# Attention over a paged cache: values gathered straight from their pages, six units turned on TensorE

## The chip, the cores and the metric

One core of a Trainium2 chip. The metric is the device time in microseconds; 3 runs of the kernel before give a median of 1006.95 us (1004.21 to 1007.05).

## The reference

Two residual layers on x (8 batches, 128 positions, 512 channels, float32):

```python
x = x + einsum('bsi,boi->bso', x, weight[adapter_ids])       # layer 0
q, k, v = x @ Wq.T, x @ Wk.T, x @ Wv.T                       # 32 q heads, 8 k/v heads, D = 128
q, k = rope(rmsnorm(q)), rope(rmsnorm(k))
kc, vc = k_cache[block_table], v_cache[block_table]          # 16 pages of 32 keys for each batch
scores = q . [kc, k] / sqrt(D), masked from cache_seqlens on
out = softmax(scores) . [vc, v]
x = x + out @ Wo.T
```

The page table, the adapter numbers and the cache lengths are inputs, known only on the chip. Each batch sees 512 cached keys and 128 new ones.

## The kernel before

**Units.** A unit u is one k/v head and one batch: hk, b = divmod(u, 8), 64 units. A unit has 4 query heads (g = 0 to 3), 640 keys (5 tiles t of 128) and two 512 x 512 weight products. Every float32 product is made as three products of float32r halves: a rounded upper part (ScalarE, a copy; names in h) and what is left (VectorE or GpSimd, a subtraction; names in l).

**Periods.** The program is written out by hand as a software pipeline. In period i TensorE makes `scores(i, g)`, projects q and k/v of unit j = i+1, multiplies the probabilities of unit w = i-1 by the values (`times_v`) and projects the output of unit o = i-2 (`project_o`). The order on each engine is the order of the calls. The first loop (periods -1 to NA) also has layer 0's products for batches 1 to 7. S, the PSUM tensor of the scores, is single, so `scores(i, g+1)` waits for `largest(i, g)`.

**Turning the probabilities.** Units below NA = 8 are normed and turned by 20 TensorE transposes (`turn_p`), and `p_hi`, `p_lo` split them out of PSUM. From unit 8 on the probabilities are cut into an upper float16 plane (`upper_plane`, ScalarE) and a lower one (`lower_plane`, VectorE, four per unit; g = 2 and 3 come one period later), and SP's DMA transposes turn both; `p_hi` (ScalarE) and `p_lo` (GpSimd, L591) read the turned planes. The last unit is turned on TensorE again.

**Keys and values.** Units 0 to NL-1 = 8 take keys straight from the pages with 16 DMAs each (`load_kt`) and values with 4 indirect DMAs of 64 KB each from GpSimd's queue (`gather_v`, L562). For the rest SP and ScalarE copy pages into an internal HBM tensor `cache_rows`, keys and values of the heads still to come, 16 pages per batch, at the pace of COPY_SP and COPY_ACT (groups of 4 pages for each period). `load_k` and `load_v` read from it, 256 KB each. From unit 8 on keys and values have one buffer, since the other half of `raw` holds the upper planes.

**GpSimd's order in a period of the second loop:** a weight split if one is due (`split_w(i, 0)`), `keys_lo(j)` (L570, kl), `q_sum(j)` (L617, m: the two rope products added, after which TensorE's `turn_q(j)` may start), `values_hi(w)` (L602, vh), `scales(j)` (L632 and L635, var and rst), `values_lo(w)` (L570, vl), three `p_lo`, a weight split if due (`split_w(i, 1)`, L570, wl), two `p_lo`.

**VectorE's order there:** `largest(i, 0)` (L1052), `lower_plane(w, 2)` (L1080), `q_products(j)` (L1115, L1119), `lower_plane(w, 3)`, `largest(i, 1)`, `output_lo`, the new value and key parts, `largest(i, 2)`, `k_sum` (L1150, waits for `scales`), `lower_plane(i, 0)`, `q_lo`, `largest(i, 3)`, the new key, `lower_plane(i, 1)`, `add_output` (L1166).

**SP's order there:** the second pair of transposes of unit i-1, the mask, weights, page copies (L338), `load_v(i)` (L443), the first pair of transposes of unit i, each released by the planes that it turns (L458, L470). The periods in which GpSimd has a split in slot 0 and in slot 1 come from the table LO_POOL and repeat with every head.

## Time and profile before

| | |
|---|---|
| median of 3 runs | 1006.95 us |
| profiled execution, first to last instruction | 1006.6 us |
| TensorE busy | 994.3 us (99%) |
| VectorE busy | 861.5 us (86%) |
| ScalarE busy | 810.3 us (80%) |
| GpSimd busy | 795.8 us (79%) |
| DMA queue of SP and ScalarE's copies and loads (q1) | 143.20 MB, 68.9% of 16 engines' span |

The page gives no time of the profiled execution other than its span; the median of the runs lies 0.35 us above it. Busy time is a mean over the whole span. The second loop makes up more than 800 us of it, with the same work in nearly every period, so one or two of its periods, read instruction by instruction, stand for it. A recorded duration includes the time that an instruction waited inside its engine for a port.

### The profile page before, as it was taken

The page shows a single profiled execution, that of the slowest core. Times are in us where ns is not written, and L with a number is a line of the kernel's source. Part 1 is how long each engine was busy: PE and PEld are TensorE (multiplying, and loading weights), DVE is VectorE, ACT ScalarE, POOL GpSimd, SP SyncE. Part 2 cuts the span into 40 slices and gives each one's busy share as a digit, 9 for nine tenths or more (in the row PEclk, how much of TensorE's full clock was granted, in tenths as well). Part 3 has the DMA queues.
Part 4 walks back from the last instruction along what each step waited for, and adds up shares of the span by engine and source line. Part 5 has one row for each costly group of instructions (what it writes and reads, how often), then busy time and mean ns, then how long its engine had stood idle before and what let it go on. Part 6 is the DMA issues. An engine that isn't in the chain of part 4 may idle for free.

```text
span 1006.6 us, 19441 instructions
## 1 busy us (share of the span) xinstructions
PE 994.3 (99%) x5471; PEld 864.3 (86%) x5471; DVE 861.5 (86%) x1787; ACT 810.3 (80%) x2109; POOL 795.8 (79%) x811
## 2 busy tenths in 40 slices
PE   8999999999999999999999999999999999999998
PEld 6778888888888888888888888888888888888886
DVE  7676657799999899999998999899999999998995
ACT  4455456698889889888988898898888988988884
POOL 4876677497889879897898888898798978888672
PEclk9999999999999999999999999999999999999999
DMA  8999879899988888888988888888988879888873
GB/s 254 277 262 260 283 229 258 213 211 201 221 162 162 161 158 153 166 157 152 171 153 162 156 160 165 148 168 155 170 148 165 157 151 166 162 162 144 153 149 84
DMA packets 513643, 180.94 MB, mean 180 GB/s; under 512 B 429873, under 2 KB 495682, under 8 KB 513538
## 3 DMA queue, kind: packets, MB, share of 16 engines
q1 hardware_dynamic: 381280, 143.20, 68.9%
q10 hardware_dynamic: 131106, 34.15, 15.3%
q0 software_dynamic: 1152, 2.36, 0.8%
q8 instruction: 45, 0.74, 0.3%
q14 instruction: 60, 0.49, 0.2%
HBM read 105.45 MB, written 31.86 MB: 136 GB/s over the span
## 4 chain that ended last, share of the span: by engine, by line
PE 95%; DVE 2%; ACTq 1%; issue 1%; ACT 1%; another core or an unknown queue 0%; POOL 0%; DVEq 0%
PE S L1408 22%; PE O L1341 7%; PE O L1343 7%; PE O L1342 7%; PE Q L1341 6%; PE Q L1343 6%; PE Y L1341 6%; PE Q L1342 6%; PE Y L1343 6%; PE Y L1342 6%; PE T L1347 4%; PE KV L1342 3%; PE KV L1341 3%; PE KV L1343 3%; PE KV L1361 1%; PE Y L1361 1%
## 5 line engine op out<-in xcount | busy, mean ns | idle before, releaser
L1080 DVE SCALAR_TENSOR_TENSOR pr<-pr,rc,raw 128x640 f16<-128x640 f32 x220 | 258.8, 1177 | 15.3 <-ACT raw L817 8.3
L1052 DVE CUSTOM_DVE_ANT_0 pr<-S,mask,rst 128x640 f32<-128x640 f32 x256 | 225.4, 881 | 16.6 <-PE S L1408 13.3
L837 ACT ACTIVATE pr<-pr,nb 128x640 f32<-128x640 f32 x256 | 211.7, 827 | 14.5 <-DVE nb L1052 14.5
L817 ACT ACTIVATE raw<-pr,rc 128x640 f16<-128x640 f32 x220 | 176.2, 826 | 0.6 <-DVE rc L1068 0.4
L617 POOL TENSOR_TENSOR m<-m 128x512 f32<-128x512 f32 x63 | 112.5, 1786 | 73.7 <-DVE m L1119 69.8
L591 POOL TENSOR_SCALAR ptl<-first 128x512 fp32r<-128x512 f16 x140 | 111.8, 799 | 17.6 <-issue 6.0
L570 POOL TENSOR_TENSOR kl<-raw,kh 128x512 fp32r<-128x512 f32 x64 | 97.8, 1528 | 34.5 <-ACT kh L720 33.5
L1408 PE MATMUL S<-kh,qh 128*128 128x320 f32 x512 | 120.8, 317 | 3.7 <-DVE nb L1052 3.6
L591 POOL TENSOR_SCALAR ptl<-turned 128x512 fp32r<-128x512 f16 x135 | 108.3, 802 | 11.2
L1408 PE MATMUL S<-kh,ql 128*128 128x320 f32 x512 | 116.8, 309 | 0.0
L783 ACT ACTIVATE Q<-Q 128x128 f32<-128x128 f32 x256 | 68.2, 266 | 59.9 <-DVE m L1119 59.9
L1408 PE MATMUL S<-kl,qh 128*128 128x320 f32 x512 | 116.2, 308 | 0.0
L1408 PEld LDWEIGHTS S<-kh,qh 128*128 128x128 f32 x512 | 91.7, 189 | 23.8 <-issue 4.7
L1341 PE MATMUL O<-pth,vh 128*128 128x512 f32 x252 | 105.5, 419 | 0.8 <-DVE ptl L983 0.5
L1341 PE MATMUL Y<-wh,oh 128*128 128x512 f32 x252 | 104.7, 415 | 0.4 <-DVE ol L983 0.4
L1341 PE MATMUL Q<-wh,xh 128*128 128x512 f32 x256 | 101.5, 396 | 0.5 <-issue 0.5
L1343 PE MATMUL Q<-wh,xl 128*128 128x512 f32 x256 | 100.9, 394 | 0.0
L1342 PE MATMUL Q<-wl,xh 128*128 128x512 f32 x256 | 100.2, 391 | 0.0
L1342 PE MATMUL Y<-wl,oh 128*128 128x512 f32 x252 | 99.7, 395 | 0.0
L1343 PE MATMUL Y<-wh,ol 128*128 128x512 f32 x252 | 99.6, 395 | 0.0
L1343 PE MATMUL O<-pth,vl 128*128 128x512 f32 x252 | 99.2, 394 | 0.0
L1342 PE MATMUL O<-ptl,vh 128*128 128x512 f32 x252 | 98.6, 391 | 0.0
(179 smaller groups left out, 2674.9 us busy)
## 6 DMA issues: line engine op xcount, KB each, us to landing
wraw<-in_wall SPq DMA_DIRECT2D x74, 256.0 KB, 4.4
cache_rows<-in_kv ACTq DMA_DIRECT2D x80, 224.0 KB
raw<-cache_rows SPq DMA_DIRECT2D x57, 256.0 KB, 4.0
raw<-cache_rows ACTq DMA_DIRECT2D x53, 256.0 KB, 5.0
mask<-mask_rows SPq DMA_DIRECT2D x64, 128.0 KB
cache_rows<-in_kv SPq DMA_DIRECT2D x36, 224.0 KB
first<-in_lw SPq DMA_DIRECT2D x5, 1024.0 KB
cache_rows<-in_kv SPq DMA_DIRECT2D x16, 192.0 KB, 4.2
```

What stands on the lines that cost most here:

```text
L570: return e.tensor_tensor(dst, src, hi.bitcast(F32), ALU.subtract)
L591: e.tensor_scalar(ptl[:, i % 3, :].rearrange("p (g n) -> p g n", g=G), plane_tile(u, 1, t), 1.0 / PS, 1.0, ALU.mult, ALU.mult).then_inc(g_ ...
L617: e.tensor_tensor(m1[:, :, :], m1[:, :, :], m2[:, :, :], ALU.add).then_inc(q_added, 1)
L783: made = e.activation(part, part, ACT.Square, accum_out=ssq[:, j % 2, r:r + 1])
L817: e.activation(upper16[:, g, :], pr[:, slot(u, g), :], ACT.Copy, scale=rc[:, u % 2, g:g + 1]).then_inc(a_f1, 1)
L837: e.activation(pr[:, slot(u, g), :], pr[:, slot(u, g), :], ACT.Exp, bias=nb[:, u % 2, g:g + 1], scale=-1.0, accum_out=sm[:, u % 2, g:g + 1 ...
L1052: e.tensor_tensor_reduce(pr[:, slot(u, g), :].rearrange("p (a n) -> p a n", a=2), S[:, :, 0:320], mask[:, u % 2, :].rearrange("p (a n) -> ...
L1080: e.scalar_tensor_tensor(out=lower16(u, g), in0=pr[:, slot(u, g), :], scalar=rc[:, u % 2, g:g + 1], in1=upper16[:, g, :], op0=ALU.mult, op ...
L1341: e.matmul(dst, lh, rh, start=first, stop=False)
L1342: e.matmul(dst, lh, rl, start=False, stop=False)
L1343: return e.matmul(dst, ll, rh, start=False, stop=last)
L1408: made = e.matmul(S[:, a, 0:320], l[:, u % 2, qs], r[:, u % 2, 320 * a:320 * a + 320], start=first, stop=last)
```

## The change

- NA goes from 8 to 6: units 0 to 5 and the last are turned on TensorE. NL is NA + 1 = 7: units 0 to 6 take their keys straight from the pages.
- All 64 units take their values from the pages, each with one indirect DMA of 256 KB (128 rows of 2 KB: four keys' values each). `load_v` is gone.
- To fit these rows, key t of a row goes to tile t: keys, mask and values are in the order (t, page, row) in place of (page, row). The host lays the caches out so, and `keys_hi` and `keys_lo` read the raw keys in runs of eight elements.
- The copies hold keys alone, 7 heads (8 for batch 7) of 16 KB per page, with new COPY_SP and COPY_ACT.
- On GpSimd `values_hi` and `values_lo` stand ahead of `q_sum` in the second loop, and behind `q_sum`, ahead of `scales`, stands the gather for unit i, after a wait for the fourth `lower_plane` of unit i-1.
- The row numbers for the gathers are made by VectorE, one instruction for each head (`value_rows`), in periods 1 to 4.

```diff
-NL = NB + 1
-NA = 8
+NA = 6
+NL = NA + 1
-COPY_SP = (0, 1, 1, 1, 1, 1, 1, 2, 0, 1, 1, 1, 1, 1)
-COPY_ACT = (2, 2, 3, 2, 2, 3, 3, 2, 1, 0, 0, 0, 0, 0)
+COPY_SP = (0, 1, 1, 1, 1, 1, 1, 2, 2, 2, 2, 1)
+COPY_ACT = (2, 3, 3, 3, 3, 3, 0, 0, 0, 0, 0, 0)
...
         def copy_page(e, b, k, number):
-            rows = slice(2 if b >= NL - NB else 4, 2 * NK)
+            rows = slice((NL - b + NB - 1) // NB, NK)
...
-            def gather_v(v, t):
+            def gather_v(v):
+                e.wait_ge(c_kidx, v // NB + 1)
+                if v >= 2:
+                    e.wait_ge(g_vlo, v - 1 if v <= NA else v)
                 e.indirect_dma_start(
-                    out=rawv[raw_at(v)][:, t, :], out_offset=None,
+                    out=rawv[raw_at(v)].rearrange("p t d -> p (t d)"), out_offset=None, in_=vc,
+                    in_offset=bass.IndirectOffsetOnAxis(ap=kidx[:, v:v + 1], axis=0)
                 ).then_inc(d_rawv[v % 2], 16)
...
-                minus(kl[:, j % 2, 0:512], rawk[raw_at(j)], kh[:, j % 2, 0:512]).then_inc(g_kc, 1)
+                minus(tiles_of(kl[:, j % 2, 0:512]), by_tile(rawk[raw_at(j)]),
+                      tiles_of(kh[:, j % 2, 0:512])).then_inc(g_kc, 1)
...
             for i in range(NA + 1, NU + 1):
                 split_w(i, 0)
                 if nxt:
                     keys_lo(j)
+                values_hi(w)
+                values_lo(w)
+                if nxt:
                     q_sum(j)
-                values_hi(w)
+                if i < NU:
+                    e.wait_ge(v_f2, G * (w - NA) + G)
+                    gather_v(i)
                 if nxt:
                     scales(j)
-                values_lo(w)
                 if w < LAST:
                     for t in range(3):
                         p_lo(w, t)
...
-                rounded(kh[:, j % 2, 0:512], rawk[raw_at(j)]).then_inc(a_kc, 1)
+                rounded(tiles_of(kh[:, j % 2, 0:512]), by_tile(rawk[raw_at(j)])).then_inc(a_kc, 1)
```

## Rows read from the trace of the kernel before

**Rows 1.** Stretches: length, then busy us (instructions) of each engine, TensorE clock, DMA.

```profile
169.12:185.84 16.72, 16.72 (x102) 14.93 (x102) 11.31 (x26) 9.61 (x30) 10.23 (x13) 1.00 0.94 267
185.84:201.72 15.88, 14.70 (x87) 12.70 (x86) 12.59 (x26) 11.68 (x29) 7.26 (x6) 1.00 0.81 169
289.10:303.62 14.52, 14.52 (x82) 12.79 (x82) 13.17 (x28) 12.34 (x32) 10.53 (x12) 1.00 0.85 156
303.62:318.14 14.52, 14.52 (x82) 12.79 (x82) 13.11 (x28) 13.17 (x34) 13.45 (x14) 1.00 0.91 172
```

**Rows 2.** Chain of waits, 160 to 180 us: start, length, what.

```profile
170.00 0.87 PE T L1347 x8
```

**Rows 3.** Who waited for whom, 230 to 970 us: total, times, longest.

```profile
POOL m L617 <- DVE m L1119: 60.9, 28, 2.3
```

**Rows 4.** SP's queue in order of time, 200 to 208 us: start, length.

```profile
204.26 2.88 SPq L338 DMA_DIRECT2D cache_rows<-in_kv  x4
```

**Rows 5.** The transposes of the lower planes (line 470): issue to landing.

```profile
DMA to landing us min/median/max: 3.3/3.4/5.3
```

**Rows 6.** The gathers (line 562): duration ns min/median/max.

```profile
L562 POOL DMA_INDIRECT raw<-in_kv,kidx x32: 943/996/1222, 12.5 to 158.8; - x32
```

**Rows 7.** GpSimd in order of time, 297 to 318 us: start, length, idle before.

```profile
297.70 1.30 POOL L570 TENSOR_TENSOR kl<-raw,kh 128x512 fp32r<-128x512 f32 x1 [0.94 <-ACT kh L720]
301.34 1.87 POOL L617 TENSOR_TENSOR m<-m 128x512 f32<-128x512 f32 x1 [2.33 <-DVE m L1119]
303.18 0.61 POOL L602 TENSOR_SCALAR vh<-raw 128x512 fp32r<-128x512 f32 x1
...
304.39 1.18 POOL L635 TENSOR_TENSOR rst<-var,mhalf 128x5 f32<-128x5 f32 x1
305.54 1.30 POOL L570 TENSOR_TENSOR vl<-raw,vh 128x512 fp32r<-128x512 f32 x1
306.92 2.48 POOL L591 TENSOR_SCALAR ptl<-turned 128x512 fp32r<-128x512 f16 x3
...
312.72 1.30 POOL L570 TENSOR_TENSOR wl<-wraw,wh 128x512 fp32r<-128x512 f32 x1
313.98 1.89 POOL L570 TENSOR_TENSOR kl<-raw,kh 128x512 fp32r<-128x512 f32 x1
315.98 1.87 POOL L617 TENSOR_TENSOR m<-m 128x512 f32<-128x512 f32 x1
```

**Rows 8.** VectorE in order of time, 298 to 318 us.

```profile
298.37 1.31 DVE L1080 SCALAR_TENSOR_TENSOR pr<-pr,rc,raw 128x640 f16<-128x640 f32 x1
...
301.18 0.88 DVE L1080 SCALAR_TENSOR_TENSOR pr<-pr,rc,raw 128x640 f16<-128x640 f32 x1
...
306.17 0.82 DVE L1150 CUSTOM_DVE_ANT_0 k<-k,rst 128x128 f32<-128x128 f32 x1
...
313.63 1.07 DVE L1080 SCALAR_TENSOR_TENSOR pr<-pr,rc,raw 128x640 f16<-128x640 f32 x1 [0.35 <-ACT raw L817]
...
315.82 0.87 DVE L1080 SCALAR_TENSOR_TENSOR pr<-pr,rc,raw 128x640 f16<-128x640 f32 x1
316.62 0.87 DVE L1052 CUSTOM_DVE_ANT_0 pr<-S,mask,rst 128x640 f32<-128x640 f32 x1
```

**Rows 9.** The sums of the rope products (line 617): duration ns min/median/max.

```profile
L617 POOL TENSOR_TENSOR m<-m x63: 1268/1868/1875, 33.4 to 969.3; 128x512 f32<-128x512 f32 x63
```

**Rows 10.** TensorE in order of time, 317 to 319 us.

```profile
317.98 0.45 PE L1408 MATMUL S<-kh,qh 128*128 128x320 f32 x2
...
318.85 0.60 PE L1347 MATMUL T<-ident,m 128*128 128x128 f32 x4
```

**Rows 11.** ScalarE in order of time, 312 to 315 us.

```profile
312.24 0.63 ACT L720 ACTIVATE kh<-raw 128x512 fp32r<-128x512 f32 x1
312.76 1.55 ACT L817 ACTIVATE raw<-pr,rc 128x640 f16<-128x640 f32 x2
```

**Rows 12.** GpSimd's products for the rope tables (line 646): duration ns.

```profile
L646 POOL TENSOR_TENSOR tab<-acc x3: 1015/1017/1036, 28.2 to 31.4; 128x384 f32<-128x384 f32 x3
```

More of the change, by code:

```diff
@@ L24 @@
 PSZ = 32
+VK = 4
+ROWS = PSZ // VK
 KEYS = 640
@@ L97, in copies_of, with build @@
             for k in range(first, first + (COPY_ACT if act else COPY_SP)[period])]
-def build(nc, x, xt, lw, wall, kv, ids_lens, table, pages, qkw, consts, iota, out):
+def build(nc, x, xt, lw, wall, kc, vc, ids_lens, table, pages, qkw, consts, iota, out):
     with ExitStack() as ctx:
@@ L157, in build @@
         il = sb("il", [P, 2 * NB], I32)
-        tabb = sb("tabb", [P, NB * NT], I32)
+        tabb = sb("tabb", [P, NB], I32)
         page = sb("page", [1, NB * NPG + NB], I32)
-        cst = sb("cst", [P, 3 + 64])
-        rowsb = cst[:, 0:3]
+        cst = sb("cst", [P, 1 + NK + 64])
+        rowsb = cst[:, 0:1]
+        first_row = cst[:, 1:1 + NK]
         ilf = sb("ilf", [P, 2 * NB])
@@ L192, in build, with by_tile, tiles_of @@
                 for n in range(2)]
+        def by_tile(keys):
+            return keys.rearrange("d (g t j) -> d t g j", g=NPG, t=NT)
+        def tiles_of(keys):
+            return keys.rearrange("d (t g j) -> d t g j", g=NPG, t=NT)
         upper16 = raw[:, 2 * HID:2 * HID + G * KEYS // 2].bitcast(F16).rearrange(
@@ L265, in build @@
         a_norm, v_norm = sem("a_norm"), sem("v_norm")
-        copy = nc.dram_tensor("cache_rows", (2 * NK, NB, NPG, PSZ * D), F32, kind="Internal").ap()
+        copy = nc.dram_tensor("cache_rows", (NK, NB, NPG, PSZ * D), F32, kind="Internal").ap()
         mask_rows = nc.dram_tensor("mask_rows", (NB, NT * P), BF16, kind="Internal").ap()
@@ L519, in _ @@
                     load_k(e, i + 2)
-                for n, (b, t) in enumerate(copies_of(i)):
-                    if n == 2 and NL <= i + 2 < NA:
-                        load_v(i + 2)
+                for b, t in copies_of(i):
                     copy_pages(b, t)
-                if len(copies_of(i)) <= 2 and NL <= i + 2 < NA:
-                    load_v(i + 2)
             for i in range(NA, NU + 2):
@@ L539, in _ @@
                     copy_pages(b, t)
-                if NL <= i < NU:
-                    load_v(i)
                 if i < LAST:
@@ L657, in _ @@
             e.wait_ge(c_mhalf, 1)
-            for t in range(NT):
-                gather_v(0, t)
-            for t in range(2):
-                gather_v(1, t)
+            gather_v(0)
+            gather_v(1)
             for i in range(-1, NA + 1):
@@ L667, in _ @@
                     values_lo(i)
[L668 to L670 removed]
+                if 1 < j <= NA:
+                    gather_v(j)
                 split_w(i, 0)
@@ L844, in _ @@
             e.dma_start(qkw_s, bc(qkw, 2 * D)).then_inc(d_small, 16)
-            for g in range(4):
-                e.dma_start(tabb[32 * g:32 * g + 32, :],
-                            table[g:g + 1, :].broadcast_to([32, NB * NT])).then_inc(d_tab, 16)
+            e.dma_start(tabb[:, :], table).then_inc(d_tab, 16)
             for c in range(6):
@@ L1198, in _ @@
             e.tensor_scalar(rnd, rnd, -1.0, HALF_PI, ALU.mult, ALU.add).then_inc(c_ang, 1)
-            key_rows()
+            table_rows()
+            value_rows(0)
             for part in range(2):
@@ L1213, in _ @@
                 turn = w >= 0
-                if i == 2:
-                    key_rows_1()
+                for hk in range(2 * i - 1, 2 * i + 1):
+                    if 1 <= hk < NK:
+                        value_rows(hk)
                 if o >= 0:
@@ L1669 @@
     p = np.arange(P)
-    consts = np.concatenate([np.stack([p, p % 32, p % 32 + 2 * 64 * PSZ], axis=1), np.broadcast_to(inv, (P, 64))],
-                            axis=1).astype(np.float32)
-    iota = np.broadcast_to(np.arange(NT * P, dtype=np.float16), (NB, NT * P))
+    rows = (p % ROWS)[:, None] + 64 * ROWS * np.arange(NK)[None, :]
+    consts = np.concatenate([p[:, None], rows, np.broadcast_to(inv, (P, 64))], axis=1).astype(np.float32)
+    iota = np.broadcast_to(np.arange(NT * P, dtype=np.float16).reshape(P, NT).T.reshape(-1), (NB, NT * P))
     arrays = {
```

76 lines of the change are left out of this document (21 added, 55 removed).

## The prediction

> **What bounds the kernel now.** I read the table by stage first. From 289 us on TensorE is busy for 14.52 of 14.52 us per unit, whether GpSimd has 10.5 or 13.5 us of work [rows 1]; a unit of the first kind, still turned on TensorE, takes 16.72. Nothing but TensorE's own work sets these stages, so a change pays only by taking work from TensorE, and costs only where it makes TensorE wait. The chain of waits says the same: its long part is one TensorE piece behind another, and the transposes stand in it with 0.87 us for eight [rows 2]. Then I read who waits on GpSimd: `q_sum` waited for VectorE 28 times between 230 and 970 us, about every second period, up to 2.3 us [rows 3]. In the other half GpSimd comes to it without a pause. Those are the periods with a split of a weight chunk ahead of `keys_lo` (slot 0 of LO_POOL, periods 8h-2, 8h-1, 8h+1, 8h+2 of head h). I call them H, the others L. After the change the second loop (periods 7 to 63) has 26 H: 9 and 10, and four for each of h = 2 to 7, thus 13 pairs.
>
> **Part 1: two units fewer turned on TensorE.** Twenty 128x128 transposes go per unit: 20 x 0.87 / 8 = 2.18 us [rows 2]; the two kinds of period differ by 16.72 - 14.52 = 2.20 [rows 1]. Units 6 and 7: -4.4 us, all on the path. The switch to the second loop moves from period 8 to 6, where VectorE has two splits of weight chunks more; its 1.2 us of TensorE idle (15.88 less 14.70, [rows 1]) stay, and VectorE's slack there (15.88 less 12.59) covers them. If it didn't, at most what GpSimd takes for two, 2.6 us [rows 7].
>
> **Part 2: copies and queues.** Keys alone: 128 page copies instead of 132, half as large. On SP periods 7 to 10 now issue eight of them ahead of `turn_upper(i, 0)` instead of four and one `load_v`. Four cost 2.88 us [rows 4], so the first transposes go out some 2.4 us later. The last one, which is waited for, is released by the fourth lower plane and goes out on time. Landing takes 3.4 us [rows 5]. ScalarE issues 12 copies in each of periods 1 to 5 where it had 8 or 12. I take 0, the cover being SP's and ScalarE's idle time there; without it +3 us, the issue time of four once more, and -1 if the lighter DMA load shortens the start.
>
> **Part 3: the gathers.** One DMA_INDIRECT holds GpSimd for 1.0 us [rows 6]. In the head four per unit become one; GpSimd doesn't set those periods, so 0. In the second loop one is added to each period, where the `load_v` that it replaces cost GpSimd nothing. The values are used almost a period later, so the landing, even at twice the 3.4 us, is hidden; the same holds for the held wait, since `q_sum` ends after the fourth lower plane anyway. Behind the gather stand `scales`, and `k_sum` on VectorE behind these.
>
> **Part 4: values_hi and values_lo before q_sum.** Here I expect the loss. Two facts first. (a) VectorE's `lower_plane` reads two SBUF tensors and doesn't run beside a GpSimd operation. At 313.63 it takes 1.07 us and ends some 0.87 after the split of 312.72 lets go; `keys_lo` at 313.98 takes 1.89 instead of 1.30, and `q_sum` 1.87, because each waits for one [rows 7, 8]; `q_sum` at its quickest is 1.27 [rows 9]. From these ends GpSimd lets go 0.19 us before its recorded end, VectorE 0.13 before its own. (b) In an H period (scores(i, 0) at 310.65) TensorE wants the row maximum of `largest(i, 1)` for scores(i, 2) at 317.98, which is there at 317.5, and q_sum for `turn_q` at 318.85, which is there at 317.85 [rows 7, 8, 10]. One period earlier the same two stand 14.52 us earlier, at 303.46 and 304.33. So the slack is 0.5 and 1.0 us, and 1.92 us (0.62 + 1.30) are put ahead of `q_sum`.
>
> The L period before it (scores at 296.13), step by step. keys_lo 297.70 to 299.00. lower_plane(w, 2) to 299.68, as now. values_hi 299.55 to 300.17. values_lo 300.24 to 301.54. lower_plane(w, 3), asked for at 301.18, runs 301.35 to 302.22. largest(i, 1) is ready at 303.0; TensorE wants it at 303.46. q_sum 302.09 to 303.38; turn_q at 304.33. No stall. Gather (0.15 of issue, then 1.05) to 304.58. scales, 1.18 and 0.33 for var and gaps (304.39 + 1.18 now comes 2.39 behind q_sum's end of 303.18, with a wait in it), to 306.09, just in time for k_sum at 306.17 [rows 8]. p_lo from 306.17 instead of 306.92.
>
> First H period. From the first p_lo to keys_lo it is 7.06 us now [rows 7], so keys_lo starts at 313.23 (kh is there at 312.86, [rows 11]) and ends at 314.53. lower_plane(w, 2) can't be asked for before 313.6, for ScalarE makes its upper plane [rows 11]. It now waits for keys_lo and runs 314.34 to 315.21. q_products to 316.41. values_hi 315.08 to 315.70, values_lo 315.77 to 317.07. lower_plane(w, 3), asked for at 316.33, waits for values_lo and runs 316.88 to 317.75. largest(i, 1) is ready at 318.54, so scores(i, 2) starts at 318.60 and not at 317.98: a stall of 0.62 us. q_sum ends at 318.91, in time for the shifted turn_q.
>
> Second H period, with scores(i, 0) at 325.79. Gather and scales end at 321.62. keys_lo is asked for at 328.76 and lower_plane(w, 2) at 328.77, a tie. If VectorE is first: keys_lo to 330.80, lower_plane(w, 3) to 331.63, values_hi to 332.12, values_lo to 333.49, q_sum to 334.85, where turn_q would be at 333.99: a stall of 0.9. If keys_lo is first, largest is late by 1.0. I take 0.92. In the L period after it everything is caught up.
>
> Sum: 13 x (0.62 + 0.92) = 20.0 us. Bounds: were the gather free, keys_lo would be held by kh (312.9) alone and the stall be 0.3 in each H, 26 x 0.3 = 8 us; were every wait short by 0.5 us against this working, nothing would be left, 0; if every H stalled like the dearer order of the tie, 26 x 1.04 = 27.
>
> The Trainium skill ("SBUF — State Buffer", SBUF: two separate sides) says that the pair of ports shared by the two engines is an exclusive lock for the whole instruction. The rows agree that it excludes, but show it let go 0.19 us early; by the page each H period would stall by some 0.2 us more, 1028 us.
>
> **Part 5: keys in another order.** keys_hi and keys_lo now read runs of eight elements. No row has such runs on GpSimd. The nearest has six runs of 64 (1.02 us for 384 elements, [rows 12]) where 384 elements at 1.30 per 512 are 0.97: 0.05 for six runs, and at most 0.5 for 64 runs. Below nothing it can't go, the elements being as many. I take 0, the nearest row's 0.05 rounded. At 0.5, each H stalls 0.5 longer (13 us), and L by some 0.1 (3 us).
>
> The Trainium skill ("GPSIMD Engine Reference", Performance pitfalls for Q7 kernels) puts a penalty of half on reads whose inner step is over 8 bytes. The step here is 4 bytes, so by the page the price is 0; the row leaves up to 0.5 open.
>
> **The sum.** 1006.6 (span) - 4.4 + 0 + 20.0 = 1022.2 us. The page gives only the span of the profiled execution; the median of the three runs lies 0.35 above it, so I predict 1022.5 us. Within 0.3%, or 3 us, of 1006.95 I call it the same, about what such a measurement can tell.
>
> **The rivals.** (A) Faster, 1002.6 us: the values fit into GpSimd's pauses in all periods. For it: in L they do, with 2.3 us of pause, and p_lo starts 0.75 us earlier, which flows into H. Against it: keys_lo can't start before kh in any case, and from there the working still leaves 0.3 us in H. It decides if waits are half a microsecond shorter than I read them. Chance 0.22. (B) About even, 1004 to 1010: stalls of 0.1 to 0.3 us per H, which take back the 4.4; it needs a gather that is nearly free or hidden. Chance 0.15, half of it within the 3 us. (C) Slower still, 1030 to 1039: reading runs of eight costs 0.3 to 0.5 us, so 1022.5 + 16 at the top. Chance 0.10. (D) That the DMA side bounds, values or transposes landing late: DMA is less loaded than before and has most of a period of slack. Chance 0.03, 1015 or more. The forecast has 0.50, its own range 1014 to 1029.
>
> **Chances and range.** Faster: 0.22 and a little of B, 0.25. Same: 0.07. Slower: 0.68. The range that holds 8 in 10 reaches over A's time on the low side and cuts C: 1002 to 1029.
>
> **What would show it.** TensorE idle before scores S<-kh, released by VectorE's nb, or before T<-ident,m, released by GpSimd's m, in H periods only: H periods of 15.1 to 15.5 us beside L periods of 14.52. The lower plane ahead of q_products near 1.6 us in H. DMA_INDIRECT near 1.0 us, kl near 1.30 uncontended. Periods 7 and 8 at 14.52 instead of 16.72. I am wrong if H periods stay at 14.52 (then A), or if L periods lengthen too (then C or D).

## The result, and the profile after

The change makes the kernel slower: 1036.75 us (median of 4 runs, 1032.45 to 1037.46) against 1005.58 us (4 runs, 1002.95 to 1007.05), a ratio of 1.0307 with a 95% interval of [1.0279, 1.0336]. The forecast, 1022.5 us in a range up to 1029, had the direction and was 14 us too low. The profiled execution took 1032.45 us with a span of 1030.7, 4.3 us below its median. The kernel before's span of 1006.6 is on the other side: executions take 1.8 us beside their span, so it stands for some 1008.4 us (an estimate), 2.8 above the median of 1005.58. So the two profiles differ by 24.1 us and the two medians by 31.2.

The first section of its page, the busy time of each engine, shows the totals:

```profile
PE 997.7 (97%) x5431; PEld 855.7 (83%) x5431; DVE 852.7 (83%) x1795; ACT 821.1 (80%) x2117; POOL 855.7 (83%) x841
```

TensorE is no longer busy in every period. These are three neighbouring stretches of the changed kernel, one L and two H periods, each from one transposition of `k` to the next (length, then busy us of each engine, as in [rows 1]):

```profile
414.91:429.44 14.53, 14.53 (x82) 12.63 (x80) 13.03 (x29) 12.36 (x33) 13.05 (x14) 1.00 0.82 145
429.44:444.90 15.46, 14.74 (x83) 12.86 (x81) 13.39 (x27) 13.76 (x37) 14.56 (x14) 1.00 0.79 166
444.90:459.96 15.06, 14.69 (x83) 12.77 (x81) 12.47 (x27) 12.90 (x34) 14.08 (x15) 1.00 0.78 163
```

The L period stands at 14.5, as L and H did before [rows 1]; the H periods take 15.46 and 15.06. GpSimd now has 13.0 to 14.6 us of work where it had 10.5 and 13.5. Who waits for whom, from 230 to 970 us (total, times, longest), has new lines:

```profile
DVE k L1126 <- POOL rst L619: 35.5, 36, 1.8
...
PEld T L1325 <- POOL m L601: 11.6, 18, 0.7
...
PEld S L1386 <- DVE nb L1028: 10.7, 17, 1.1
...
POOL raw L550 <- issue: 8.2, 50, 0.2
```

`q_sum`'s wait for VectorE [rows 3] is no longer among the long ones; TensorE waits for `q_sum`'s m, and for the row maximum's nb. VectorE waits an us for `rst` in more than every second period. GpSimd in order of time in the first of the two H periods (answers [rows 7]):

```profile
433.17 1.30 POOL L556 TENSOR_TENSOR wl<-wraw,wh 128x512 fp32r<-128x512 f32 x1
434.44 1.27 POOL L556 TENSOR_TENSOR kl<-raw,kh 128x512 fp32r<-128x512 f32 x1
435.68 1.20 POOL L585 TENSOR_SCALAR vh<-raw 128x512 fp32r<-128x512 f32 x1
436.96 1.29 POOL L556 TENSOR_TENSOR vl<-raw,vh 128x512 fp32r<-128x512 f32 x1
438.21 1.86 POOL L601 TENSOR_TENSOR m<-m 128x512 f32<-128x512 f32 x1
440.23 1.11 POOL L550 DMA_INDIRECT raw<-in_vc,kidx  x1 [0.17 <-issue]
```

VectorE beside it (answers [rows 8]):

```profile
434.63 1.76 DVE L1056 SCALAR_TENSOR_TENSOR pr<-pr,rc,raw 128x640 f16<-128x640 f32 x1 [0.89 <-ACT raw L797]
...
437.51 1.43 DVE L1056 SCALAR_TENSOR_TENSOR pr<-pr,rc,raw 128x640 f16<-128x640 f32 x1
438.86 0.87 DVE L1028 CUSTOM_DVE_ANT_0 pr<-S,mask,rst 128x640 f32<-128x640 f32 x1
```

And TensorE (answers [rows 10]), the first line from the second H period of an earlier pair:

```profile
395.11 0.65 PE L1325 MATMUL T<-ident,m 128*128 128x128 f32 x4 [0.41 <-POOL m L601]
...
439.79 0.56 PE L1386 MATMUL S<-kh,qh 128*128 128x320 f32 x2 [0.72 <-DVE nb L1028]
```

The reader is to see a chain. The lower plane asked for at 434.63 waits for `keys_lo` (1.76 instead of 0.87), the next one for `values_lo` (1.43), `largest` ends at 439.7, and `scores` starts 0.72 late.

**Where the time went.** I measure a period from one transposition of `k` on TensorE to the next, and call what it has above 14.52 us its stall. The last column runs from period 63's transposition to the end of the span. All in us, worked out from the profiled executions:

| kernel | span | period 9 begins | stalls 9 to 15 | stalls 16 to 62 | end |
|---|---|---|---|---|---|
| before | 1006.6 | 190.6 | 1.7 | 0.0 | 30.2 |
| after | 1030.7 | 189.1 | 4.3 | 19.4 | 33.8 |
| after_again | 1035.4 | 189.0 | 10.0 | 20.7 | 31.7 |
| values_first_before | 1026.9 | 189.6 | 4.6 | 18.4 | 30.2 |
| no_gather | 1020.6 | 188.1 | 3.4 | 14.7 | 30.4 |
| scales_first | 1026.2 | 188.7 | 3.9 | 17.5 | 32.1 |
| no_hold | 1032.3 | 189.3 | 7.1 | 20.7 | 31.2 |
| short_splits | 1025.5 | 188.5 | 6.4 | 14.4 | 32.1 |
| keys_straight | 1033.7 | 188.4 | 8.9 | 20.3 | 32.0 |
| turned_only | 1019.6 | 189.1 | 16.1 | 0.0 | 30.3 |
| seven_turned | 1004.5 | 191.2 | 1.9 | -2.7 | 30.2 |
| eight_turned | 1030.6 | 189.7 | 5.5 | 19.9 | 31.4 |
| gather_after_p | 1031.4 | 188.3 | 5.3 | 21.8 | 31.9 |
| copies_early | 1042.5 | 201.6 | 4.3 | 20.7 | 31.9 |
| gather_after_p_early | 1039.8 | 198.0 | 4.0 | 21.8 | 31.9 |
| q_first | 1127.0 | 191.6 | 17.0 | 100.8 | 33.5 |
| old_order | 1096.7 | 189.7 | 11.7 | 77.8 | 33.4 |
| max_first | 1121.3 | 193.6 | 13.9 | 96.3 | 33.4 |
| max_scales_first | 1054.0 | 190.4 | 10.0 | 37.5 | 32.0 |

In the profiled execution of the changed kernel the 24.1 us are -1.5 to period 9, 2.6 in periods 9 to 15, 19.4 in the 47 after, and 3.6 at the end. Within one head of the steady part the stalls are 0.6 (period 21, where ScalarE waited 0.58 us for late keys), 0.58 and 1.10 (22 and 23, H), 0.94 and 0.54 (25 and 26, H), and nothing else.

A stall in this sense is more than idle time. In the two H periods above TensorE was idle for 0.72 and 0.37 us, yet it was also busy for 14.74 and 14.69 us instead of 14.52. The first two products behind the pause, the row of 439.79, take 0.56 us where two take 0.45 without one [rows 10]; the rest of the growth I did not trace. Over the 26 H periods of the changed kernel the longer busy time makes 7.1 of 20.3 us.

And in a few places TensorE's clock fell to its lower level, 1.2 GHz. In the profiled execution of the changed kernel this was at the end, behind an idle time of 2.01 us (1010.76):

```profile
1011.20:1014.60 3.40, 3.40 (x11) 2.45 (x10) 0.36 (x1) 1.26 (x2) 2.62 (x5) 0.50 0.20 77
```

The last column but two is the granted clock, 0.50. At half the clock 3.4 us hold 1.7 us' worth of work, so some 1.7 us are lost each time (an estimate). The kernel before has one such stretch too, from 41.6 to 45.0 us (clock 0.50), behind 1.23 us of idle time; its period there took 18.36 us where the changed kernel's took 16.94.

### The profile page after: what moved, and what is told of

It reads as the page before. It is cut to its first block, busy times and chain, and to the rows that moved or that the text cites. A ratio compares the mean times of both kernels' runs of the same rounds, so it can differ in the third digit from the quotient of the medians.

```text
span 1030.7 us, 19308 instructions
## 1 busy us (share of the span) xinstructions
PE 997.7 (97%) x5431; PEld 855.7 (83%) x5431; DVE 852.7 (83%) x1795; ACT 821.1 (80%) x2117; POOL 855.7 (83%) x841
## 4 chain that ended last, share of the span: by engine, by line
PE 57%; POOL 18%; issue 8%; DMA 5%; ACT 5%; DVE 5%; ACTq 1%; SPq 0%; DVEq 0%; POOLq 0%
PE S L1386 13%; POOL ptl L577 5%; PE O L1319 4%; PE O L1321 4%; PE O L1320 4%; PE Y L1319 4%; PE Y L1321 4%; PE Y L1320 4%; POOL kl L556 3%; POOL vl L556 3%; PE T L1325 3%; PE Q L1319 3%; PE Q L1321 3%; PE Q L1320 3%; POOL wl L556 3%
## 5 line engine op out<-in xcount | busy, mean ns | idle before, releaser
L1056 DVE SCALAR_TENSOR_TENSOR pr<-pr,rc,raw 128x640 f16<-128x640 f32 x228 | 276.5, 1213 | 22.9 <-ACT raw L797 20.8
L797 ACT ACTIVATE raw<-pr,rc 128x640 f16<-128x640 f32 x228 | 182.1, 823 | 2.6 <-DVE rc L1044 2.2
L577 POOL TENSOR_SCALAR ptl<-first 128x512 fp32r<-128x512 f16 x145 | 120.0, 828 | 17.8 <-issue 4.3
L1386 PE MATMUL S<-kh,qh 128*128 128x320 f32 x512 | 122.2, 319 | 12.1 <-DVE nb L1028 11.6
L577 POOL TENSOR_SCALAR ptl<-turned 128x512 fp32r<-128x512 f16 x140 | 116.8, 834 | 12.4 <-PE O L1321 1.2
L556 POOL TENSOR_TENSOR kl<-raw,kh 128x512 fp32r<-128x512 f32 x64 | 94.0, 1468 | 36.8 <-ACT kh L700 36.8
L601 POOL TENSOR_TENSOR m<-m 128x512 f32<-128x512 f32 x63 | 102.8, 1632 | 14.1 <-DVE m L1095 14.0
```

The costliest lines, as they stand in the source:

```text
L556: return e.tensor_tensor(dst, src, hi.bitcast(F32), ALU.subtract)
L577: e.tensor_scalar(ptl[:, i % 3, :].rearrange("p (g n) -> p g n", g=G), plane_tile(u, 1, t), 1.0 / PS, 1.0, ALU.mult, ALU.mult).then_inc(g_ ...
L601: e.tensor_tensor(m1[:, :, :], m1[:, :, :], m2[:, :, :], ALU.add).then_inc(q_added, 1)
L797: e.activation(upper16[:, g, :], pr[:, slot(u, g), :], ACT.Copy, scale=rc[:, u % 2, g:g + 1]).then_inc(a_f1, 1)
L1056: e.scalar_tensor_tensor(out=lower16(u, g), in0=pr[:, slot(u, g), :], scalar=rc[:, u % 2, g:g + 1], in1=upper16[:, g, :], op0=ALU.mult, op ...
L1386: made = e.matmul(S[:, a, 0:320], l[:, u % 2, qs], r[:, u % 2, 320 * a:320 * a + 320], start=first, stop=last)
```

## The experiments

**The changed kernel once more.**

> The changed kernel once more, beside the three below. Its earlier times lie between 1032.5 and 1037.5 us and the profiled one is the shortest of them. If what differs is chance of one execution, this lies at 1036 to 1037 and its profiled execution may show where the 4 us sit; if it is a habit of the profiled execution, the profile is again 4 us below the others.

Measured: 1034.21 us (1031.87 to 1037.21), ratio 1.0268 [1.0231, 1.0305]. Its four executions fall in two groups, near 1032 and near 1037, so it is chance of one execution. The profile caught a long one, and the table shows where it is longer: 5.7 us in periods 9 to 15. There a key load issued at 248.84 was waited for until 257.85, 2.32 us by ScalarE, TensorE was idle for 2.04 us in front of 263.93, and from 264.2 to 267.6 its granted clock was 0.50: period 13 has 16.31 us of TensorE's busy time where the shorter execution has 14.78. So some 1.5 of the 5.7 us are the lower clock. The forecast of 1022.5 would be 10 us below the short group.

**GpSimd's order.** Three kernels: the gather's kernel with `q_sum` first, with the old order, and the kernel before with the values first.

```
q_first (changed kernel)      old_order (changed kernel)   values_first_before
 keys_lo                       keys_lo                      keys_lo
+q_sum                        +q_sum                       -q_sum
 values_hi; values_lo          values_hi                    values_hi
-q_sum                        +scales                      +values_lo
 gather_v                      values_lo                   +q_sum
 scales                       -q_sum                        scales
                               gather_v                    -values_lo
                              -scales
```

> The changed kernel with q_sum ahead of values_hi and values_lo (keys_lo, q_sum, values_hi, values_lo, gather, scales). Theory O (order: what stands ahead of q_sum makes TensorE wait for m, and VectorE's lower plane waits for values_lo, so that the row maximum is late): m's waits go and most of nb's; 15 to 20 us come back, 1016 to 1022. Theory G (the gather's time on GpSimd makes the stalls, whatever stands where): less than 5 us come back, over 1031. What is left in either case: the head and the end, some 6 us that the sum had at nothing, and the periods 5 mod 8, where the keys land late (0.6 each).

> The changed kernel with GpSimd's old order (keys_lo, q_sum, values_hi, scales, values_lo) and the gather behind values_lo, still held until the fourth lower plane. Theory O: as q_first or a little better, since scales come 2.4 us earlier: stalls of the second loop of 0 to 5 us, thus 1008 to 1014. Theory G: GpSimd has 13.5 + 1.1 us of work in H periods against 14.52, so that stalls of 0.3 or more in each of the 26 H stay, 1018 or more.

> The kernel before with nothing changed but GpSimd's order: values_hi and values_lo ahead of q_sum. Theory O as the prediction had it with a free gather: 0.3 us in each of 26 H periods, 8 us, thus 1013 to 1015. If the order alone makes all the stalls (gather free): 20 us, 1026. Theory G: under 3 us, the gather being absent.

Measured: q_first 1124.93 us, ratio 1.117 [1.1132, 1.1208]; old_order 1099.01 us, 1.0925 [1.0893, 1.0956]; values_first_before 1028.33 us, 1.0221 [1.0189, 1.0253]. The third says that the order alone makes most of the loss, 21 us of the 27 to 31. The first two say what I had not thought of: without that order, and with the gather right behind `values_lo`, the kernel is 92 to 118 us above the one before. (In q_first some 17 us of it are the lower clock, granted 0.50 in ten stretches of 3.4 us.) Both theories were wrong on them. In old_order nearly every period of the second loop takes 16.1 to 16.2 us, L as well as H. GpSimd there:

```profile
603.52 1.87 POOL L601 TENSOR_TENSOR m<-m 128x512 f32<-128x512 f32 x1
605.37 0.61 POOL L585 TENSOR_SCALAR vh<-raw 128x512 fp32r<-128x512 f32 x1
606.29 0.20 POOL L616 TENSOR_SCALAR var<-ssq 128x5 f32<-128x5 f32 x1 [0.31 <-ACT KV L768]
606.57 1.21 POOL L619 TENSOR_TENSOR rst<-var,mhalf 128x5 f32<-128x5 f32 x1
607.77 1.30 POOL L556 TENSOR_TENSOR vl<-raw,vh 128x512 fp32r<-128x512 f32 x1
609.88 1.11 POOL L550 DMA_INDIRECT raw<-in_vc,kidx  x1 [0.81 <-POOL vl L556]
611.07 3.86 POOL L577 TENSOR_SCALAR ptl<-turned 128x512 fp32r<-128x512 f16 x5
```

It is a closed loop, and the chain of last releasers shows which: TensorE's K/V projection, ScalarE's sum of squares (KV L768), `scales`, `values_lo`, the gather, `p_lo`, and TensorE again, whose `times_v`, scores and Q stand ahead of the next K/V projection. Two rows show it, from 230 to 1000 us and from 230 to 970 us: TensorE waited for ptl 94 times, 55.3 us in all, and `scales` for ScalarE 46 times, which is nearly every period. `q_sum` and `values_hi` are not in it: they had ended 0.31 us before. The gather adds its 1.11 us, 0.81 in which it waits for GpSimd's own `values_lo`, and 0.08. Take these 2.0 from 16.13 and the same loop without the gather has some 14.13 us (an estimate), 0.4 below TensorE's 14.52. gather_after_p below bears it out: it has the same order with the gather later, behind the third `p_lo` and so outside this loop, and its undisturbed periods take 14.5. The change's order takes `values_lo` out of the loop and puts the gather ahead of the point where `scales` waits. That is what makes room for the gather, and it is paid with the H stalls.

**The gather, the hold, the scales and the split.**

```
no_gather:     -gather_v(i) of the second loop
scales_first:  +scales(j)
                wait_ge(v_f2, ...); gather_v(i)
               -scales(j)
no_hold:       -wait_ge(v_f2, G * (w - NA) + G)
short_splits:   slot 0, second loop: tensor_scalar(wl, w_raw, 1.0, 1.0, mult, mult)
```

> The changed kernel without the gathers of the second loop (units 7 to 63; the values of the units from 7 on are left out, old rows stand in their place). In the kernel before with the values moved ahead, the first p_lo waited some 0.8 us in every period though no gather was there. Theory O2 (the order alone sets the stalls of the second loop, the gather runs in that pause): H periods at 15.2 as there, L at 14.52; the stall of periods 5 mod 8 (late keys, 0.6 each) and the 3.7 us at the end go with the gather; 1028.3 less 4.4 for the two units, and up to 2 for the head: 1024 to 1027. Theory G2 (the gather's 1.1 us is what makes GpSimd late in H): H at 14.8 or less, 1010 to 1015.

> The changed kernel with scales ahead of the gather, everything else as it is. VectorE's k_sum waited for rst 37 times, 36.9 us in all. If that wait is on the path of the late row maximum (theory K), scores' waits for nb shrink and 5 to 10 us come back, 1025 to 1030. If nb is late only through the lower planes that wait for values_lo and keys_lo (theory L), nothing changes but the place of the gather against the key load: 1032 to 1035. The gather lands 1.5 us later, which hides.

> The changed kernel without the gather's wait for the fourth lower plane (it still waits for values_lo of its buffer). The prediction took the wait as free. If it is, the same within 0.3% in the second loop (the idle time before the gather is 0.17 us with it), and at most 2.7 us back at the end, where the last gather waited so long: 1031 to 1035. If the hold keeps the gather clear of the transposes and the key loads, the time gets longer: 1038 or more.

> The changed kernel, in which the split of a weight chunk ahead of keys_lo (slot 0, second loop) is one copy of the chunk, 0.62 us instead of 1.30 (so the lower weights of those chunks are left out). Theory H (the split ahead of keys_lo is what makes H periods late): each H stall of 0.55 to 1.10 shrinks by about 0.6, 26 x 0.6 = 15 us, 1018 to 1022. Rival (H periods are late for their second weight chunk or for VectorE's load): under 5 us, 1029 or more.

Measured: no_gather 1022.89 us, ratio 1.0179 [1.0151, 1.0206]; scales_first 1027.70, 1.0236 [1.0196, 1.0275]; no_hold 1033.79, 1.0271 [1.0238, 1.0305]; short_splits 1029.04, 1.0248 [1.0204, 1.0292].

no_gather comes 1 us below what theory O2 said, and in the way that it said: H periods at 15.17 and 15.20, the L of the late keys back at 14.52, the end at 30.4. So a free gather does not leave 0.3 us in each H, as the prediction's working had it, but 0.65 to 0.69. Who waits, from 230 to 970 us, in that kernel, its two H periods, and TensorE's pause in the first of them:

```profile
POOL ptl L577 <- issue: 32.5, 49, 2.1
...
PE S L1382 <- DVE nb L1024: 11.0, 25, 0.8
```

```profile
426.62:441.78 15.16, 14.77 (x83) 12.85 (x80) 12.74 (x27) 13.69 (x37) 13.25 (x13) 1.00 0.74 139
441.78:456.98 15.20, 14.74 (x82) 12.88 (x80) 12.87 (x27) 12.89 (x34) 13.61 (x14) 1.00 0.68 127
```

```profile
430.07 1.30 POOL L556 TENSOR_TENSOR wl<-wraw,wh 128x512 fp32r<-128x512 f32 x1 [0.50 <-ACT wh L696]
431.32 1.27 POOL L556 TENSOR_TENSOR kl<-raw,kh 128x512 fp32r<-128x512 f32 x1
...
436.69 0.56 PE L1382 MATMUL S<-kh,qh 128*128 128x320 f32 x2 [0.39 <-DVE nb L1024]
```

Two things make up the difference to 0.3. First, `keys_lo` starts 4.70 us behind the transposition of `k`, where the working had it start with `kh` at 4.44 (312.9 less 308.46, the transposition in the kernel before). In the first H a split stands ahead of it which waited 0.50 us for ScalarE's wh. In the second GpSimd works without a pause from its first `p_lo` on, and this `p_lo` does not start when GpSimd is free: 49 times a first `p_lo` waits, 0.7 us on average. The row names no engine; it is the turned lower planes, for VectorE's fourth lower plane ends at 435.82, the transposes behind it take 3.4 us [rows 5], which makes 439.2, and `p_lo` starts at 439.35. So time that a missing gather frees is idle. Second, the pause itself costs more than its length: scores(i, 2) starts at 10.07 instead of 9.52 behind the transposition, and its first two products take 0.56 us instead of 0.45 [rows 10]. 0.55 and 0.11 are the 0.66 of the period. With the gather the H pair costs 1.5 to 1.7 us instead of 1.35.

scales_first has VectorE's waits for `rst` down from 35.5 us to 7.6 (23 waits, 230 to 970 us). Its 1027.70 us lie in theory K's range, but its ratio's interval overlaps after_again's, so whole runs show no gain for sure. Of the 4.5 us of span that it is below the changed kernel, 1.9 are in periods 16 to 62, 0.4 before period 9, 0.4 in periods 9 to 15, and 1.8 at the end, where the changed kernel's profile has the stretch at the lower clock and this one hasn't. In the steady part one stall goes and another comes: the second H of the pair ahead of a head's first period takes 15.13 instead of 15.62 and the L of the late keys 14.5 instead of 15.1, but the first H of that pair takes 15.4 instead of 15.1 and the L two periods ahead of it 14.88 instead of 14.5. TensorE waits less for nb and more for m (24 waits, 10.4 us, instead of 18, 6.9 us, 230 to 970 us). no_hold changes nothing (its interval and after_again's are one), as the prediction had said. short_splits answers the H question halfway: 0.68 us less ahead of `keys_lo` leaves 0.45 to 0.6 in each H, in which TensorE waits for the row maximum alone (nb, 26 times, 8.6 us from 290 to 960 us, and not once for m). The likely reason is the same two lower planes, which still stand behind `keys_lo` and `values_lo`. The 15 us that I expected were 5 in the trace's periods 16 to 62, and in whole runs the interval overlaps after_again's.

**VectorE's order, the units and the keys.**

```
max_first:        largest(i, 1) ahead of lower_plane(w, 3) on VectorE
max_scales_first: that and scales_first
turned_only:      kernel before, NA = 6, NL = 7, the changed kernel's COPY_SP and COPY_ACT
keys_straight:    by_tile(keys) = keys.rearrange("d (t g j) -> d t g j", g=NPG, t=NT)
```

> The changed kernel with VectorE's largest(i, 1) ahead of lower_plane(w, 3) in the second loop. Theory L (TensorE waits for a row maximum that is late only because it stands behind a lower plane that waits for GpSimd's values_lo): the maximum comes 0.7 us earlier, scores no longer wait for nb, and 5 to 9 us come back, 1025 to 1029; what is left is the wait for m in H periods and the late keys. Rival (q_sum is as late, so that m takes over every stall): less than 2 us back.

> Both: VectorE's largest(i, 1) ahead of lower_plane(w, 3), and GpSimd's scales ahead of the gather (which alone gave 1027.7). If the two gains add: 1018 to 1023. If both took away the same wait: 1026 or more.

> The kernel before with the first part of the change alone: six units turned on TensorE, and the copy schedule that goes with it (whole pages of keys and values are still copied, GpSimd's order is the old one). If the two units are worth what the prediction said and the earlier switch costs nothing: 4.4 us less, 1001 to 1003. If the head gives back half of it, as in the changed kernel's trace: 1004 or more. The copies move twice the bytes of the changed kernel in the same few periods, so the keys of the first periods of the second loop may be late; then the periods 7 to 15 show it.

> The changed kernel with keys_hi and keys_lo reading the keys as they lie, in 512 running elements instead of runs of eight (so the keys of a unit stand in another order than its mask and its values). If the runs cost nothing, as keys_lo at 1.29 us says: the same within 0.3%. If they cost ScalarE or GpSimd something that the medians hide: up to 5 us less.

Measured: max_first 1115.96 us, ratio 1.1057 [1.1009, 1.1105]; max_scales_first 1056.37, 1.0495 [1.0452, 1.0538]; turned_only 1021.31, 1.0129 [1.0091, 1.0168]; keys_straight 1032.90, 1.0241 [1.0204, 1.0278].

max_first is the clearest miss. The maximum came earlier, but the fourth lower plane later, and behind it stand the transposes, the gather and `p_lo`. Who waited in it, 290 to 960 us:

```profile
POOL ptl L577 <- issue: 65.7, 27, 4.6
...
PE O L1319 <- POOL ptl L577: 40.8, 34, 3.6
```

So the late row maximum can't be mended there: the same VectorE slot feeds both chains. Some 14 of the 109 us above the kernel before are the lower clock, 0.50 in eight stretches of 3.4 us behind such waits. keys_straight is no different from after_again: the order of the keys costs nothing measurable.

max_scales_first has the same trouble in a milder form, with 28 us more of span than scales_first. turned_only runs from period 13 on without a stall, and has 16 us of them in periods 9 to 12, 14 more than before. In SyncE's queue there:

```profile
189.55 6.29 SPq L338 DMA_DIRECT2D cache_rows<-in_kv  x8
195.95 0.55 SPq L443 DMA_DIRECT2D raw<-cache_rows  x1
196.59 3.65 SPq L458 DMA_TRANSPOSE first<-raw  x1
```

Eight copies and the value load go out ahead of the transposes, and the first `p_lo` waited up to 4.6 us, 15.6 us in four waits (160 to 250 us); the row names no engine, and I take it for these transposes. TensorE waited for ptl 11.8 us, in five waits. Behind two of them, of 3.14 and 3.47 us, the clock was 0.50 for 3.4 us each, so some 3 of the 16 us are the lower clock (TensorE's busy time in these two periods is 16.28 and 16.51 us instead of 14.8).

**The gather outside the loop, and the copies early.**

```
gather_after_p: keys_lo; q_sum; values_hi; scales; values_lo; 3 x p_lo; gather_v(i); split_w(i, 1); 2 x p_lo
copies_early:   COPY_SP = (0, 2, 2, 3, 3, 3, 2, 0, 0, 0, 0, 0)
```

> The changed kernel with SyncE's page copies all in periods 1 to 6 (COPY_SP 2, 2, 3, 3, 3, 2 there and none from period 7 on). Theory C (the eight copies that SyncE issues ahead of the transposes in each of periods 7 to 11, 6.3 to 7.4 us, and the DMA load of 1.0 in them, make keys and transposes land late): the stalls of periods 9 to 15 fall from 4.3 to 10.0 us to what the order makes, about 3, the times scatter less, 1028 to 1031. If the first loop can't take the copies (its DMA share was 0.77), its periods get longer and the head gives it back: 1033 or more.

> The changed kernel with GpSimd's old order (keys_lo, q_sum, values_hi, scales, values_lo, three p_lo) and the gather behind the third p_lo, ahead of the second split. Theory P (what costs is what stands in the chain from TensorE's Q to the first p_lo; before it had 0.4 us to spare there, with the gather behind values_lo it had 16.13 a period): nothing is added to the chain, keys_lo comes 1.1 us later in H periods, where q_sum still ends before 10.85 us after turn_k; the second loop runs at 14.52 or up to 14.7 in H, thus 1003 to 1010 with the trouble of periods 9 to 15. Theory G (1.1 us more of GpSimd work is what H can't take): H at 15.0 and more, 1020 or more.

> Both: the gather behind the third p_lo in GpSimd's old order, and SyncE's page copies in periods 1 to 6. If both theories hold: 999 to 1004, below the kernel before. If the copies are what the first loop can't take: 1005 or more.

Measured: copies_early 1044.25 us, ratio 1.0356 [1.0312, 1.0399]; gather_after_p 1033.23, 1.0258 [1.0211, 1.0304]; gather_after_p_early 1041.95, 1.0339 [1.0295, 1.0384].

gather_after_p takes the gather out of the loop and out of the values' order, and costs the same, 25 us: theory P fell, and theory G, which has the time right, had no reason for it. GpSimd of that kernel, and VectorE beside it:

```profile
431.15 1.09 POOL L550 DMA_INDIRECT raw<-in_vc,kidx  x1 [0.28 <-issue]
432.27 1.32 POOL L556 TENSOR_TENSOR wl<-wraw,wh 128x512 fp32r<-128x512 f32 x1
```

```profile
431.47 2.81 DVE L1054 SCALAR_TENSOR_TENSOR pr<-pr,rc,raw 128x640 f16<-128x640 f32 x1 [0.17 <-ACT raw L795]
434.20 0.67 DVE L1140 TENSOR_TENSOR acc<-acc,Y 128x512 f32<-128x512 f32 x1
```

The lower plane, 0.87 us by itself, took 2.81: it began 0.32 us behind the start of the gather and got through only when the split behind the gather let go (434.28 less 0.87 is 433.41, 0.18 ahead of the split's end). This happens to 18 lower planes of this kernel, in periods 9 and 13 and then in three of every eight (1, 4 and 6 mod 8), and these periods have 16.7 of the 21.8 us of stalls from period 16 on. The next maximum, and TensorE's scores with it, are late: TensorE waited for nb 44 times, 11.6 us (290 to 960 us), and periods of 15.56 and 15.0 stand beside 14.5.

It is not the gather by itself that holds the lower plane. In the same kernel 36 lower planes began 0.1 us behind the start of a gather and took 0.87 to 0.89 us, and in scales_first all 55 that began beside a gather, 0.34 us behind its start or later, took 0.88 or 0.89. One of each, VectorE above GpSimd, first gather_after_p, then scales_first:

```profile
446.97 0.87 DVE L1054 SCALAR_TENSOR_TENSOR pr<-pr,rc,raw 128x640 f16<-128x640 f32 x1
446.90 1.11 POOL L550 DMA_INDIRECT raw<-in_vc,kidx  x1 [0.28 <-issue]
```

```profile
411.54 0.88 DVE L1056 SCALAR_TENSOR_TENSOR pr<-pr,rc,raw 128x640 f16<-128x640 f32 x1 [0.16 <-ACT raw L797]
411.18 1.17 POOL L550 DMA_INDIRECT raw<-in_vc,kidx  x1 [0.19 <-issue]
```

The 18 that were held have in common a late start beside the gather and a split right behind it; which of the two operations holds them from the start on, no run here shows.

copies_early does what theory C said in periods 9 to 15 (4.3), and gives back 12 in periods 7 and 8: eight copies went out from 162.10 to 171.79 ahead of the first transposes, VectorE waited 7.6 us for these, and TensorE 5.9 for VectorE's row maximum; from 182.4 to 189.2 us the clock was 0.50 as well, which makes some 3 of the 12. I had put copies into period 6, which is the first with transposes on SyncE; the misplacement is mine, and a schedule that ends in period 5 wasn't tried.

**How many units.**

```
seven_turned: kernel before, NA = 7; COPY_SP = (0, 1, 1, 1, 1, 1, 1, 2, 1, 1, 1, 1, 1)
eight_turned: changed kernel, NA = 8; COPY_SP = (0, 1, 1, 1, 1, 1, 1, 2, 1, 1, 1, 1)
```

> The kernel before with seven units turned on TensorE instead of eight, and copies spread as they were (two more page groups behind period 8, one fewer in all). If one unit is worth 2.2 us and the copies fit: 1002 to 1004 where before is 1005 to 1007. If the earlier switch takes it back, as with six: 1006 or more. Had the stalls of six units (16 us) come from the switch itself, seven would show half of them, 1010 or more.

> The changed kernel with eight units turned on TensorE as before, and copies of keys spread over as many periods as before. Theory E (the early switch is bad beside the copies, whose stalls of 2 to 10 us in periods 9 to 15 it makes): 4.4 us more for the units and 3 to 7 less for the stalls, 1031 to 1035, with less scatter. If the two units are a clean gain: 1037 to 1040.

Measured: seven_turned 1008.30 us (10 runs) against 1006.38 (13), ratio 1.0018 [1.0001, 1.0036]; eight_turned 1032.36 us, 1.0250 [1.0214, 1.0286]. Neither shows a gain from fewer units: one unit less saves nothing in the kernel before (period 8 there took 19.7 us, 3 more than in the kernel before; its later periods stand at 14.46 and not 14.52, which is the -2.7 of the table and which I can't explain: it isn't the chip, for eight_turned on the same one has 14.52), and undoing the two in the changed kernel costs nothing (its interval overlaps after_again's). Theory E holds in direction. No kernel here beats the one before; scales_first has the lowest ratio of those with the gather, but not clear of eight_turned's, short_splits' or keys_straight's. (The chips differ: the kernel before takes 1004.65 us at the median on one and 1008.20 on another, so the ratios compare kernels, not the times.)

## Why the prediction was too low

**What bounds the kernel, and the H and L periods: right in the main.** H rose to 15.06 to 15.62 where 15.1 to 15.5 was written, by waits for nb and for m. L periods stayed at 14.5 except one in each head (5 mod 8), which rose to 14.6 to 15.7 for its late keys: the sign that the prediction gave for rival D, in one L of four. GpSimd lets go 0.19 us before its recorded end here too: 434.63 + 1.76 - 0.87 = 435.52, and `keys_lo` ends at 435.71. The Trainium skill ("SBUF — State Buffer", SBUF: two separate sides) has the lock held for the whole instruction; this row, like those of before, has it let go early.

**Part 4, the H stalls: right in sum, and partly by luck.** The 26 H periods of the profiled execution have 20.3 us of stalls where 20.0 was the sum, but not as worked out, 0.62 by nb and then 0.92 by m in each pair. In periods 25 and 26 it is 0.94 by nb and 0.54 by m; in 22 and 23 it is 0.58 by m and 1.10 by both. The working left out what a pause costs beyond its length (7.1 of the 20.3 us), and had the pauses themselves too long (13.1 us of idle time); the two errors cancel.

**The failed bound in it: "were the gather free ... 26 x 0.3 = 8 us".** no_gather has 0.65 to 0.69 in each H and 18.0 us of stalls; values_first_before has 23.0, of which 1.7 are the switch's that the kernel before has too. The working let `keys_lo` start with kh and counted the pause alone; it starts 0.27 us later, behind a split that waits for ScalarE or a `p_lo` that waits for the transposes, and the pause costs 0.1 more. So rivals A and B, 0.37 of the chance, rested on a slack that wasn't there. With 0.67 in each H, 1006.6 - 4.4 + 17.4 = 1019.6 is what a free gather gives by the prediction's own sum (no_gather's span is 1020.6), and the low end should have been near that, not 1002.

**The step that failed: what the sum took as nothing because something else covers it.** These are the key loads (no term at all), "I take 0" in part 2 for head and copies, and the end (no term).

**Late keys: 3.4 us instead of nothing.** The L periods 5 mod 8 have 1.20, 0.62, 0.10, 0.60, 0.51 and 0.34 us of stalls (13 to 53). A key load on ScalarE's queue now goes out with a gather and takes 6.0 us at the median to land, where it took 5.0. Without the gathers, in no_gather, these periods stand at 14.5 again. In the longer execution of after_again the L periods have 9.0 us.

**Part 1, -4.4 us: right for the two units.** Periods 7 and 8 went from 33.4 to 30.7 us, -2.8, with a switch in period 7 that costs 1.6; the kernel before has its switch in period 9, 1.7 us, and the changed kernel hasn't. That makes -4.5. **The head, "I take 0": 2.6 us more.** Ahead of period 7 the changed kernel is 1.2 us later, though the kernel before lost 1.4 us there to the lower clock: it starts 1.1 us later, spends 1.0 more in period 2 and 0.8 in period 5. eight_turned has neither of the last two, so in the profiles it begins period 9 only 0.6 us behind the changed kernel. I didn't isolate these; ScalarE's copies, and transfers that land late in the start, are the candidates. In whole runs nothing of the gain of part 1 can be measured: seven_turned's ratio is 1.0018 and eight_turned's interval overlaps after_again's.

**Part 2 and part 3's queues in periods 9 to 15: a matter of the execution.** Their stalls are 2.6 to 8.3 us above those of the kernel before, which includes the H stalls there. SyncE puts out up to eight copies ahead of the transposes, with the DMA engines busy at 0.98 to 1.01 of their time in periods 9 to 11, and keys land late. In after_again this makes 5.7 us against the profiled execution here (1.5 of it by the lower clock), more than the 4.3 by which the median lies above it. That it is the copies is what turned_only (16 us in the same periods, gone when they end) and copies_early (no copies there, and four executions within 1.0 us of one another instead of 5) point to; copies_early's 4.3 us of stalls in these periods are no fewer than in the shorter execution of the changed kernel.

**The end, nothing: 1.5 to 3.6 us.** GpSimd in the last periods of the changed kernel:

```profile
1004.44 1.11 POOL L550 DMA_INDIRECT raw<-in_vc,kidx  x1 [2.72 <-DVE pr L1056]
1009.87 2.96 POOL L577 TENSOR_SCALAR ptl<-first 128x512 fp32r<-128x512 f16 x4 [4.33 <-issue]
```

The last gather goes out beside the last transposes of unit 62, issued at 1004.18; `p_lo` starts 5.7 us later, where they take 3.4 to land [rows 5], and TensorE's `O` waits with it (2.01 us idle at 1010.76). Behind this pause the clock is 0.50 for 3.4 us, as shown above, and that is some 1.7 of the 3.6 us. after_again has 1.10 and 1.17 us of idle time in two pauses there, no stretch at the lower clock, and an end of 31.7. no_gather has the old 30.4.

**Part 3's gather: 1.10 us instead of 1.0 (median of 64, 0.96 to 1.16), landing 5.6 at the median where 6.8 was allowed: right.** So is part 5: `keys_lo` takes 1.29 us at the median and 1.31 before. The Trainium skill ("GPSIMD Engine Reference", Performance pitfalls for Q7 kernels) has no penalty for an inner step of 4 bytes; keys_straight agrees.

**The sum of the misses.** Late keys 3.4 us, the H stalls 0.3, the head 2.6, the end 3.6, less 0.1 in part 1 and less the 1.4 that the lower clock had cost the kernel before: 1022.2 + 8.4 = 1030.6, the span of the profiled execution but for 0.1. Above it 1.8 of time beside the span, of which I had added 0.35 (1032.45 against 1030.7, as in every execution; the span of 1006.6 was that of a long execution), and 4.3 to the median: 14.2 in all. Of the 14, the terms set to nothing make 9.6, and chance of the profiled executions, before and after, most of the rest. The range's top, 1029, was cut out of rival C, though most terms taken as nothing could only add.

## What to carry to other kernels

When an operation is put into an in-order queue, find the closed loop that passes through its place (here the K/V projection, its sum of squares, scales, `values_lo`, `p_lo`, TensorE) and compare its length with the period: a place with 0.4 us of slack turned 2.0 us into 1.6 us of every period, while in the change's place the gather costs some 9 in all (the ratios of no_gather and after_again), beside the 21 of the order that makes the place. Take the loop from the chain of releasers, not from the longest waits: `q_sum`'s long wait for VectorE was not in it. Time freed ahead of a wait for a DMA is not gained, so take who-waits-for-whom after every "would start earlier". Count a pause of TensorE at more than its length, and look at the granted clock behind each long one. Where many terms are set to zero because something covers them, let the range go out on their side.

## What the runs showed of the hardware that I had not expected

- A lower plane of 0.87 us took 2.8 when it began 0.3 us into a gather with a split right behind it (18 times in gather_after_p), but 0.88 or 0.89 beside a gather in all 55 cases of scales_first, and 0.87 to 0.89 in 36 cases of gather_after_p that began 0.1 us into it.
- A gather that waits for GpSimd's own operation just before it starts 0.81 us after that operation's recorded end (42 times, 34.2 us, in old_order from 230 to 1000 us); with `q_sum` between, the pause was 0.17.
- A pause of TensorE costs more than its length: with 0.39 us of idle time the period grew by 0.65, and TensorE's busy time from 14.52 to 14.77 (no_gather).
- Behind some pauses the granted clock was 0.50 (1.2 GHz) for 3.4 us: behind 2.01 us in the changed kernel's end, 2.04 in after_again, 3.14 and 3.47 in turned_only, but not behind 2.62 us in turned_only (228.64); in q_first it fell ten times, behind pauses of 0.9 to 1.4 us.
- A 256 KB gather lands 5.6 us after its issue at the median (3.7 to 7.6), and `p_lo` could start only 5.7 us behind a transpose issued 0.26 us ahead of one, where a transpose lands in 3.4 us at the median.
- The eight executions of the changed kernel fall into two groups 4 to 5 us apart (1032 and 1037). In the one pair of profiles the longer one is longer in some 100 us where copies, key loads and transposes share DMA engines busy at up to 1.0.
